# Zero-weight products in the slots of a vision tower's round, and selection weights padded to 128 rows

## What is computed

```python
h = window_attention(x)                 # 8 x 8 windows, 8 heads of 8, 2-D rotary codes, projection
h = h + mamba(layernorm(h))             # per image a scan along its 4096 tokens:
#   x_branch, z = split(rmsnorm(.) @ in_proj); x_branch = silu(causal conv of 4 taps)
#   dA = exp(delta * A);  h_t = dA_t * h_(t-1) + (x_branch * delta)_t * B_t
#   y_t = sum over 16 states of h_t * C_t, + x_branch * D, * silu(z), @ out_proj
h = h + experts(layernorm(h))           # router, top 2 of 6 experts, each of three layers
```

## Time and profile before

| | |
|---|---|
| median of 3 runs | 1922.06 us (1921.57 to 1926.98) |
| the profiled execution | 1921.26 us |
| its span, first to last instruction | 1919.4 us |
| mean granted TensorE clock | 0.74 of full speed |
| PE busy / PEld busy | 1368.6 us (71%) / 612.8 us (32%) |
| DVE busy | 1353.5 us (71%) |
| ACT busy | 1035.8 us (54%) |
| POOL busy | 1207.9 us (63%) |
| DMA, queue of SP | 302.10 MB, 57.1% of 16 engines' span |

### The profile page before, as it was taken

The page is one execution under the profiler, slowest core; times in us unless marked ns, Lnnn a source line. Parts: engine busy times, 40 slices in busy tenths (PEclk is TensorE's granted clock), DMA queues, the critical chain, the costliest instruction groups (busy, mean ns, idle before and its releaser), DMA issues. The chain is left out here.

```text
span 1919.4 us, 26560 instructions
## 1 busy us (share of the span) xinstructions
PE 1368.6 (71%) x8212; PEld 612.8 (32%) x8212; DVE 1353.5 (71%) x1834; ACT 1035.8 (54%) x1909; POOL 1207.9 (63%) x1666
## 2 busy tenths in 40 slices
PE   3675676776869687786968777685968777666565
PEld 1443242241515233141524324151524324121111
DVE  1114697778687877778697777868687777878941
ACT  2244556465655657465665646565655646554432
POOL 2205676667576766757676676757676675877651
PEclk9877777786877677686868778687867768576755
DMA  2005595657566564755666565765666575677820
GB/s 63 15 1 148 143 266 140 188 149 201 165 162 192 154 179 139 207 166 167 178 174 181 139 195 151 202 166 163 197 157 176 143 199 169 196 195 205 221 73 6
DMA packets 215205, 303.80 MB, mean 158 GB/s; under 512 B 79436, under 2 KB 79640, under 8 KB 214936
## 3 DMA queue, kind: packets, MB, share of 16 engines
q1 hardware_dynamic: 215064, 302.10, 57.1%
HBM read 274.75 MB, written 20.97 MB: 154 GB/s over the span
## 5 line engine op out<-in xcount | busy, mean ns | idle before, releaser
L1273 POOL TENSOR_TENSOR hc<-hs,c_rep 128x512 f32<-128x512 f32 x512 | 649.7, 1269 | 406.7 <-DVE hs L1024 406.4
L1024 DVE TENSOR_TENSOR_SCAN hs<-bank,state,xd 128x512 f32<-128x512 f32 x512 | 651.7, 1275 | 55.7 <-issue 49.3
L776 ACT ACTIVATE bank<-dl,a_neg 128x512 f32<-128x512 f32 x512 | 351.0, 687 | 371.7 <-DVE hs L1024 363.1
L1015 DVE TENSOR_TENSOR xd<-xd,bank 128x512 f32<-128x512 f32 x512 | 337.0, 663 | 101.1 <-PE bank L429 100.9
L544 PE MATMUL bank<-q_diag,k_heads 128*128 128x128 f32 x1024 | 206.1, 327 | 6.4 <-ACT top_row L769 4.9
L439 PE MATMUL bank<-hc,wts 128*32 128x512 f32 x1024 | 199.9, 843 | 5.9 <-POOL hc L1273 5.4
L544 PEld LDWEIGHTS bank<-q_diag,k_heads 128*128 128x128 f32 x1024 | 174.8, 212 | 73.3 <-issue 63.5
L705 PE MATMUL bank<-e,wts 64*64 64x512 f32 x384 | 84.2, 960 | 129.9 <-ACT e L956 129.9
L532 PE MATMUL bank<-k_heads,q_diag 64*64 64x512 f32 x512 | 92.2, 797 | 102.7 <-DVE neg_max L1044 70.6
L1044 DVE TENSOR_REDUCE neg_max<-bank 128x8 f32<-128x512 f32 x128 | 86.9, 687 | 103.8 <-PE bank L532 103.3
L1345 POOL TENSOR_TENSOR ew<-ew,e 128x512 f32<-128x512 f32 x96 | 121.0, 1261 | 33.5 <-ACT e L769 33.5
(11 more groups left out here) (171 smaller groups left out, 2416.2 us busy)
## 6 DMA issues: line engine op xcount, KB each, us to landing
xd<-xdel_rows SPq DMA_DIRECT2D x512, 256.0 KB, 4.0
dl<-delta_rows SPq DMA_DIRECT2D x512, 256.0 KB, 3.7
delta_rows<-delta SPq DMA_DIRECT2D x16, 512.0 KB, 7.3
xdel_rows<-xdel SPq DMA_DIRECT2D x16, 512.0 KB, 4.0
xin<-in_x_dram SPq DMA_DIRECT2D x32, 128.0 KB, 2.5
q_diag<-rot SPq DMA_DIRECT2D x64, 64.0 KB
out_dram<-res SPq DMA_DIRECT2D x256, 16.0 KB
k_heads<-rot SPq DMA_DIRECT2D x128, 16.0 KB
```

Source lines behind the costliest of these rows:

```text
L776: act.activation(decay_ps[n % 2][:, :], dl[:, n % 4, :], ACT.Exp, scale=a_neg[:, g:g + 1])\
L1015: dve.tensor_tensor(xd[:, n % 8, :], xd[:, n % 8, :], b_ps[:, :], ALU.mult).then_inc(injected.sem, 1)
L1024: dve.tensor_tensor_scan(hs[:, n % 4, :], decay_ps[n % 2][:, :], xd[:, n % 8, :], state[:, g:g + 1], ALU.mult, ALU.add).then_inc(scanned.s ...
L1273: pool.tensor_tensor(hc[:, n % 8, :], hs[:, n % 4, :], c_rep[:, BAND * h:BAND * h + BAND], ALU.mult)\
```

## The change

It adds a tile of zeros (128 x 128, bf16) and a table of slots, `FILLERS`. In the listed slots of the rounds 0 to 15, PE begins the slot with that many products of the zeros, as weights, with 512 columns of `top_sel` (bf16, ones and zeros); they are added to `y_ps` while its sum is open, so they add zero. That is 31 products in a round, 496 in all, none with a wait or a semaphore. The tiles `w_sel` and `wT` get 128 rows instead of 24, the new ones zero, so that L673 multiplies over 128 rows. `eb3_2`'s product still takes 24. Setup clears one more tile on POOL and `wT` on DVE.

```diff
+FILLERS = {7: 4, 8: 5, 11: 5, 16: 1, 23: 6, 24: 1, 25: 1, 26: 5, 27: 2, 30: 1}
...
-        w_sel = sb("w_sel", [4 * E, 2 * EP, 128], F32R)
+        w_sel = sb("w_sel", [128, 2 * EP, 128], F32R)
...
+        zeros = sb("zeros", [128, 128], BF16)
...
-        wT = sb("wT", [4 * E, 512], F32R)
+        wT = sb("wT", [128, 512], F32R)
...
+            def keep_busy(n):
+
+                for _ in range(FILLERS.get(n, 0)):
+                    pe.matmul(y_ps[:, :], zeros[:, :], top_sel[:, 0:8, :], start=False, stop=True, skip_group_check=True)
...
-                        pe.matmul(use.bank[64 * s:64 * s + 64, :], eb3_2[:, s, :], wT[:, :].bitcast(F32),
+                        pe.matmul(use.bank[64 * s:64 * s + 64, :], eb3_2[:, s, :], wT[0:4 * E, :].bitcast(F32),
...
                 for n in range(SLOTS):
                     k, s = attention_at(c, n)
+                    if has(c):
+                        keep_busy(n)
...
-                    copy(wT[:, :], use.bank[0:4 * E, :]).then_inc(use.drained, 1)
+                    copy(wT[0:4 * E, :], use.bank[0:4 * E, :]).then_inc(use.drained, 1)
...
-            dve.tensor_copy(w_sel[:, :, :], staging[0:4 * E, 0:2 * EP * 128].rearrange("p (a b) -> p a b", a=2 * EP))\
+            dve.tensor_copy(w_sel[:, :, :], staging[:, 0:2 * EP * 128].rearrange("p (a b) -> p a b", a=2 * EP))\
                .then_inc(setup_dve, 1)
+            dve.memset(wT[:, :].bitcast(F32), 0.0).then_inc(setup_dve, 1)
...
-            pool.memset(staging[0:4 * E, :], 0.0).then_inc(setup_pool, 1)
+            pool.memset(staging[:, :], 0.0).then_inc(setup_pool, 1)
             pool.memset(q_diag[:, :, :], 0.0).then_inc(setup_pool, 1)
             pool.memset(top_row[:, :], 0.0).then_inc(setup_pool, 1)
+            pool.memset(zeros[:, :], 0.0).then_inc(setup_pool, 1)
```

More of the change, by code:

```diff
@@ L757, in _ @@
             pe.wait_ge(placed, 192)
-            pe.wait_ge(setup_dve, 10)
-            pe.wait_ge(setup_pool, 14)
+            pe.wait_ge(setup_dve, 11)
+            pe.wait_ge(setup_pool, 15)
             pe.wait_ge(setup_act, 3)
@@ L1003, in _ @@
             act.wait_ge(placed, 192)
-            act.wait_ge(setup_pool, 14)
-            act.wait_ge(setup_dve, 10)
+            act.wait_ge(setup_pool, 15)
+            act.wait_ge(setup_dve, 11)
             rounds(body)
@@ L1227, in _ @@
             dve.tensor_scalar(z_w[:, :], col("z_in"), col("normw"), None, ALU.mult).then_inc(setup_dve, 1)
-            dve.wait_ge(setup_dve, 6)
+            dve.wait_ge(setup_dve, 7)
             dve.tensor_tensor(conv_w[:, 1, :], conv_w[:, 0, :], col("conv_tap", 128, 256), ALU.mult)\
                .then_inc(setup_dve, 1)
-            dve.wait_ge(setup_dve, 8)
+            dve.wait_ge(setup_dve, 9)
             dve.tensor_tensor(conv_w[:, 0, :], conv_w[:, 0, :], col("conv_tap", 0, 128), ALU.mult)\
@@ L1235, in _ @@
             dve.tensor_copy(h_bias[:, :], b_ps[:, 0:C]).then_inc(setup_dve, 1)
-            dve.wait_ge(setup_dve, 10)
-            dve.wait_ge(setup_pool, 14)
+            dve.wait_ge(setup_dve, 11)
+            dve.wait_ge(setup_pool, 15)
             rounds(body)
@@ L1366, in _ @@
             for half in range(2):
-                pool.wait_ge(setup_pool, 4 + half)
+                pool.wait_ge(setup_pool, 5 + half)
                 pool.memset(v_diag[64 * half:64 * half + 64, :, :, 9 * half + 8:9 * half + 9], 1.0)\
                     .then_inc(setup_pool, 1)
-            pool.wait_ge(setup_pool, 7)
+            pool.wait_ge(setup_pool, 8)
             pool.memset(state[:, :], 0.0).then_inc(setup_pool, 1)
@@ L1373, in _ @@
                 pool.memset(eps[:, i:i + 1], v).then_inc(setup_pool, 1)
-            pool.wait_ge(setup_pool, 14)
-            pool.wait_ge(setup_dve, 10)
+            pool.wait_ge(setup_pool, 15)
+            pool.wait_ge(setup_dve, 11)
             rounds(body)
```

## The result

| | before | after |
|---|---|---|
| median | 1921.82 us (1921.21 to 1926.98, 4 runs) | 1892.78 us (1891.26 to 1909.17, 4 runs) |
| profiled execution / span | 1921.26 / 1919.4 us | 1909.17 / 1907.4 us |
| mean granted clock | 0.74 | 0.79 |
| PE busy | 1368.6 us | 1406.5 us |
| idle before `feed`, for the B row | 100.9 us | 62.8 us |

The changed kernel is faster by 1.4% (ratio of the means 0.9859, 95%: 0.9809 to 0.9908); by the medians it is 29.0 us, 1.5%. The forecast was 1880 us, a gain of 2.2%; the measured median lies 12.8 us above it, within the range of 1852 to 1908.

The account below looks back on a forecast made before the run. It took PE's low clock in slots 25 to 29, delaying the B row DVE needs, as the reachable bound. 12 rounds x 3.2 us plus 3 x 1 us made 41.4 us off, hence 1880 us, range 1852 to 1908.

Parts of the forecast that it names:

- The bound and the place of the gain: End of the round: DVE waits 6.91 us for the B row from slow PE, the wait the change can reach.
- Part 1: Each product of zeros costs PE 0.43 us at the low clock level, some 0.22 us at the high one.
- Those cost nothing: Zeros in slots 7, 8 and 11 lie before PE's idle waits of 2.49 and 1.59 us, so cost no time.
- Part 2: Padding L673 to 128 rows costs zero; at the other end, 3.9 us a round at the high level.
- Part 3: Zeros and padded L673 keep the high clock through slots 23 to 31; POOL limits the gain to 3.2 us a round.
- rival C: Clock rises only after slot 27 or falls between slots 24 and 25: 0 to 1.5 us a round, 1903 to 1922; chance 0.13.
- the whole next round moves: PE is dense from slot 31 to slot 7 at full clock, so the next round comes 3.2 us earlier.
- POOL's hand-over: Slots 29 and 31: `layer3` needs POOL's fourth and sixth products, limiting the gain to 2.6 to 4.0 us a round.
- Setup and edges: Setup costs zero, at most 0.5 us; round 0 gains nothing, rounds 13 to 15 gain 1 us each.
- Rival A: Slots 25 to 31 stay at the low clock with nine products more: up to +48 us, or 1963 us; chance 0.14.
- Rival B: Slots 20 to 22 might also run fast: up to 3.2 us a round more, 1842 us; chance 0.13.

Follow-up runs that it names:

- e1: The changed kernel with the padding to 128 rows kept and all 31 products of zeros left out; 1888.98 us, ratio 0.9839.
- e5: The changed kernel without the zeros of slots 23 to 30, keeping the padding and the zeros of slots 7, 8, 11 and 16; 1880.26 us.
- e10: As e6, but without the early zeros of slots 7, 8, 11 and 16; 1885.09 us, ratio 0.9823.
- e6: The changed kernel with six zeros in slot 24 and three in slot 25 instead of one each, none in slot 30; 1875.82 us.
- e9: As e6, but POOL multiplies only 256 of the 512 columns of each expert product; 1856.38 us, ratio 0.9667.
- e8: As e6, plus three zeros in slot 20 behind a wait for ACT's filled sum; 1869.92 us, ratio 0.9733.
- e11: As e6, but with the selection weights and `wT` at 24 rows again; 1876.20 us, ratio 0.9766.
- e4: The changed kernel with its 31 zero products on 32 rows and 32 columns of the array instead of 128 x 128; 1918.10 us, ratio 0.9991.
- e2: The changed kernel with all 31 products of zeros kept but the selection weights left at 24 rows; 1927.47 us, ratio 1.0029.
- e7: As e1, plus three zeros in slot 20 behind a wait for ACT's filled sum; 1888.27 us, ratio 0.9822.

## Why the prediction was right, and where it was not

- **The bound and the place of the gain: right.** The wait for the B row fell by 38.1 us (100.9 to 62.8), the time from the first scan to the end by 24.2; the rest went to other waits of DVE. In the view of waits, those for L526 (`hid`, slots 9 to 12) grew from 18.8 to 26.2 us and those for the scores from 103.3 to 106.2 us.
- **Part 1, the price of a zero: right** (0.31 us on average, about 0.3 forecast; five take 1.25 us at the high level and 2.36 us at the low one, the last one's passage included). From the first to the fifth that is 0.22 and 0.43 us each, as forecast. With 512 columns each, that is 2.4 and 1.2 columns a ns; the forecast's "2.4 GHz" and "1.2 GHz" are names of these two levels, 1.00 and 0.50, and no trace shows a frequency. Four times the 0.06 and 0.11 us of the rows would be 0.24 and 0.44, a slip of rounding. "Those cost nothing" for the early ones was right as a cost, but they also give: 8.7 us (e1 against e5) and 9.3 us (e10 against e6). With them the low level takes 6 us in place of 10 to 11 of the stretch from 20 to 44 us after the first scan (5.7 in after, 6.3 in e5, 6.5 in e6; 10.1 in before, 10.6 in e1, 11.1 in e10; but 9.1 in e9, which has them too and half of POOL's weighting). I had considered the early slots for their cover only.
- **Part 2, the padding: the price was right, its worth was not seen.** The forecast costed the padded L673 at zero, and named it beside the zeros as keeping the clock. It did not ask what it would do alone. It does the whole of it: six products on 128 rows instead of 24 take 32 us off (e1), at 0.80 us each at the low level where they took 0.79.
- **Part 3 is where the forecast failed, in two steps.** The first: "I take it that the full-array zeros and the padded L673 keep the clock at 2.4 GHz through slots 23 to 31". It fell in slot 24, after its scores, at the place that rival C named, for 3.4 us in five rounds and 10.2 us in seven. The size of the gain was right where the low stretch was short: from the `hc` of slot 25 (POOL, 1020.11 there, 1018.12 in before) PE reaches slot 31's `layer3` after 15.73 us instead of 18.91, which is 3.2 us, and the B row's product after 13.13 instead of 16.94, 3.8 us; 3.2 and 4.0 were forecast. With the long one it is 16.95 and 15.05 us (from 910.92 on): 2.0 and 1.9 us. The mean over all 12 rounds is 2.6 us (19.01 to 16.41), so this step explains 0.6 us of the 1.5 us a round that are missing.
- **The second step that failed is "the whole next round moves".** Slots 0 to 24 took 91.42 us in after and 90.48 before, which is the other 0.9 us. DVE's longer waits for L526 and the scores, 10.3 us in all, are about as much as these 12 times 0.9. In e6 the same part takes 90.45 us, so the step held there. Why it did not hold in after was not traced; the places of the clock's changes in these slots differ from round to round (below). Rival C had 0 to 1.5 us a round; the profiled rounds gave 1.66.
- **POOL's hand-over: right as a bound, reached in a part of the rounds only.** With the clock held (e6) the late part is 3.3 us shorter than before (3.2 forecast), the interval 106.15 us and the median 1875.8; the forecast had 106 and 1880. The late part is 15.70 to 15.72 us in e6, e8, e10 and e11 alike, and only less work on POOL (e9) made it shorter. Its working is thus borne out, for another kernel than the changed one.
- **That the median came so near is partly luck.** The forecast credited the late zeros with the gain and the early ones with nothing. By the medians the padding gave 32.0 us, the early zeros 8.7 us on top of it (e5), and the late zeros cost 12.5 us (after against e5).
- **Setup and edges: right.** PE's first attention product starts at 18.12 us (18.11 before). Round 0 and the rounds after 12 gave 4.2 us, 3 forecast.
- **Rival A was wrong in its first mechanism**: with products of zeros the late slots stood at 1.00 (e6, e11), where without them they were low for 10.2 or 13.6 us (e1). Its second, busy time, does not describe the late slots (e4), where narrow zeros did not help (0.50 at 12.87 of 13.60 us busy); in the early slots narrow and whole-array zeros did the same (6.3 us low in e4 and in e5). Still, its cost was the fate of the late zeros of this change: the zeros alone (e2) are slower than nothing by 0.3%. **Rival B** in its form (slots 20 to 22 turning fast by themselves) did not happen: their mean clock in rounds 1 to 12 is 0.62 in before and 0.60 in after. With zeros placed there (e8, 0.69) DVE's wait shrank by about 1.1 us in most rounds, and the interval by 0.5 us where the rival had up to 3.2.

## What to carry to other kernels

Where TensorE runs at its low level although it is busy, look first for products that use few rows of the array and can be padded to 128 at the same number of streamed columns. Here that cost nothing measurable (0.80 us a product instead of 0.79) and gave 32 us (e1), while added products in a dense stretch cost their columns at the low level where they failed to lift it, 0.43 us each; the late ones of this change cost 12.5 us (after against e5). If products are added, try first the slots where PE idles anyway: the early ones here gave 8.7 us. Filling the gaps ahead of the dense stretch held the level through it, but brought only 4.4 us more (e6 against e5), because the next engine in the chain, POOL, already set the time (with half of its weighting, e9, the time fell by 19.4 us). And measure each part alone: the sum hid that one group of zeros gave and the other cost.

## What the runs showed of the hardware that was not expected

**The clock in the run-in differs between executions.** The instructions ahead of round 0 on PE are the same before and after, and so is their start, but in the profiled execution of after the first attention is slower. PE's groups from 53 to 74 us, after and then before:

```profile
L555 PE MATMUL bank<-top_row,top_sel 128*128 128x128 bf16 x24 | 7.5, 314 | 0.0
```

```profile
L546 PE MATMUL bank<-top_row,top_sel 128*128 128x128 bf16 x32 | 7.6, 237 | 0.0
```

The same products take 314 ns on average instead of 237, 24 of them fit where 32 did, and the first scan is 12.2 us later. The changed kernel's other three runs lie at 1891 to 1894 us, 15 to 18 us below the profiled one, so a few us more than the run-in explains. The first scan lies at 177 to 180 us in before and in eight of the experiments, at 184.7 in e7, 188.3 in e10 and 190.9 in e5, and e6, whose instructions ahead of round 0 are those of after, has it at 178.1. Two of e5's six runs lie some 12 us above the other four (1892 against 1879 to 1880). The clock's first record is a high level: it begins 57.2 us after the span's start in before and 56.4 to 58.9 us in the eight experiments, 73.1 us in after, and 72.6, 73.0 and 80.0 us in e5, e7 and e10. L555 takes 314 ns ahead of it and 219 ns behind it in after. Why the clock rises later in some executions was not found.

**The clock's changes lock to the round, or wander.** In nine of the rounds 1 to 12 of before the interval is 109.1 to 109.4 us; in e5, e6 and e8 the last rounds with attention have 105.8 us each, although the late slots are at the high level throughout in two of these kernels and not in e5, and in e6's the clock falls and rises at the same six places of the round in the last three of the rounds 1 to 12 (30.7, 37.5, 47.7, 61.4, 68.2 and 81.9 us after the first scan). In after the places and the intervals (105.9 to 109.4 us) change from round to round. My reading is that a group of zeros was worth some 9 us through where it put the later changes (e5 against e1: 0.2 us a round in the late part, 0.5 us in slots 0 to 24); no run shows how it does so.
